# Narrow attentions: TensorE makes the scores of the batch three ahead in the middle of its slot, behind the first half of the product with the values, and no longer at the slot's end

## What is computed

```python
def attention(q, k, v, mask):
    scores = jnp.einsum('bhqd,bhkd->bhqk', q, k) / jnp.sqrt(jnp.float32(HD))
    scores = scores * mask - 10000.0 * (1.0 - mask)
    probs = jax.nn.softmax(scores, axis=-1)
    return jnp.einsum('bhqk,bhkd->bhqd', probs, v)
...
x = hidden_states + attn_out
ln_out = layernorm(x, ln2_s, ln2_b)
q = ln_out @ w_q + b_q
kv = encoder_states @ w_kv + b_kv
...
x = x + cross_out
```

## Time and profile before

| | |
|---|---|
| median of 3 runs | 2136.84 us |
| the profiled execution: its time, its span | 2138.01 us, 2136.3 us |
| TensorE matmuls busy (share of the span) | 1944.2 us (91%) |
| VectorE, ScalarE, GpSimd busy | 1261.8, 1085.0, 516.4 us |
| mean granted TensorE clock | 0.96 |
| first group of slot 0, last half of a product with the values, on TensorE, start | 40.66 us, 357.66 us |

### The profile page before, as it was taken

The page is one execution under the profiler, slowest core; times in us unless marked ns, Lnnn a source line. Parts: engine busy times, 40 slices in busy tenths (PEclk is TensorE's granted clock), DMA queues, the critical chain, the costliest instruction groups (busy, mean ns, idle before and its releaser), DMA issues. The chain is left out here.

```text
span 2136.3 us, 40585 instructions
## 1 busy us (share of the span) xinstructions
PE 1944.2 (91%) x15496; PEld 1692.5 (79%) x15496; DVE 1261.8 (59%) x2546; ACT 1085.0 (51%) x2920; POOL 516.4 (24%) x346
## 2 busy tenths in 40 slices
PE   6999996999999999999899999999988986898974
PEld 4677764997999999999699999999978984566653
DVE  6888886235645555555465555555552364888883
ACT  3787877545443344443453344334446543566653
POOL 3555453544200000000240000000005514324220
PEclk9999998999999999999999999999998997899986
DMA  5000001300000000002200000000020000000000
GB/s 188 2 2 2 2 2 42 117 1 6 6 6 5 0 5 5 5 5 90 74 6 1 5 5 5 5 0 5 29 89 1 1 1 1 1 11 6 6 11 10
DMA packets 29534, 40.72 MB, mean 19 GB/s; under 512 B 1923, under 2 KB 21477, under 8 KB 29157
## 3 DMA queue, kind: packets, MB, share of 16 engines
q1 hardware_dynamic: 29412, 39.06, 5.4%
HBM read 32.76 MB, written 2.10 MB: 16 GB/s over the span
## 5 line engine op out<-in xcount | busy, mean ns | idle before, releaser
L761 DVE TENSOR_TENSOR w_head_lo<-banks,w_head_hi 128x512 fp32r<-128x512 f32 x128 | 88.1, 691 | 249.5 <-ACT w_head_hi L673 241.9
L692 ACT ACTIVATE arena<-banks 128x512 f32<-128x512 f32 x128 | 74.9, 597 | 295.1 <-PE banks L551 291.0
L727 DVE TENSOR_TENSOR arena<-banks,cols 128x512 f32<-128x512 f32 x128 | 88.6, 692 | 227.0 <-PE banks L118 226.8
L470 POOL TENSOR_TENSOR w_hT_lo<-arena,w_hT_hi 128x512 fp32r<-128x512 f32 x16 | 20.9, 1306 | 821.0 <-ACT w_hT_hi L647 821.0
L685 ACT ACTIVATE arena<-banks,arena 128x129 f32<-128x129 f32 x512 | 181.3, 376 | 39.5 <-DVE arena L741 39.5
L964 POOL TENSOR_TENSOR arena<-arena 128x1024 f32<-128x1024 f32 x64 | 150.4, 2373 | 162.2 <-DVE arena L1250 162.2
L673 ACT ACTIVATE w_head_hi<-banks 128x512 fp32r<-128x512 f32 x128 | 76.5, 598 | 196.1 <-PE banks L561 196.0
L1168 ACT ACTIVATE arena<-arena 128x128 f32<-128x128 f32 x512 | 163.5, 397 | 1.8 <-DVE arena L1259 1.6
L116 PE MATMUL banks<-w_wo_lo,w_head_hi 128*128 128x256 f32 x512 | 148.6, 290 | 1.3 <-DVE w_head_lo L761 1.3
L116 PE MATMUL banks<-w_hT_lo,w_hi 128*128 128x256 f32 x512 | 146.6, 286 | 0.0
L116 PE MATMUL banks<-w_kv_lo,w_hi 128*128 128x256 f32 x512 | 145.2, 284 | 0.2
(11 more groups left out here) (299 smaller groups left out, 5702.9 us busy)
## 6 DMA issues: line engine op xcount, KB each, us to landing
arena<-in_L_xattn_wq SPq DMA_DIRECT2D x8, 512.0 KB, 4.9
arena<-in_L_xattn_wk SPq DMA_DIRECT2D x8, 512.0 KB, 6.0
arena<-in_L_xattn_wv SPq DMA_DIRECT2D x8, 512.0 KB, 6.9
arena<-in_L_xattn_wo SPq DMA_DIRECT2D x8, 512.0 KB, 9.5
arena<-ctx_t SPq DMA_DIRECT2D x16, 256.0 KB, 2.5
x<-in_x SPq DMA_DIRECT2D x4, 512.0 KB, 6.6
ctx_t<-in_ctx_t SPq DMA_DIRECT2D x1, 2048.0 KB, 11.7
arena<-in_L_xattn_w SPq DMA_DIRECT2D x2, 1024.0 KB, 12.8
```

Source lines behind the costliest of these rows:

```text
L692: act.activation(probT[:, b, :, :], bank[5 + b][:, :].rearrange("p (h q) -> p h q", h=HG), ACT.Copy).then_inc(probT_ok, 1)
L727: dve.tensor_tensor(qT[:, h:h + 2, :], bank[use % 2][:, :].rearrange("p (h t) -> p h t", h=2), core.col(bias, g * HG + h, 2)[:, :, None].t ...
L761: dve.tensor_tensor(head_lo[:, two, :], bank[5 + half][:, :].rearrange("p (h t) -> p h t", h=2), head_hi[:, two, :], ALU.subtract).then_in ...
```

## The change

In TensorE's slot `scores(n + 3)` moves from the last place to the place behind `weigh_values(n, 0)`. Nothing is added or removed, and the lists of the other engines are the same.

```diff
                 prob_transpose(n, 2)
                 weigh_values(n, 0)
+                if n + 3 < NU:
+                    scores(n + 3)
                 if even and r + 2 < NR:
                     project_q(r + 2, 1)
                 if not even and r + 2 < NR:
...
                 prob_transpose(n, 3)
                 if not even and r + 2 < NR:
                     project_v(r + 2, 1)
-                if n + 3 < NU:
-                    scores(n + 3)
```

## The result

| | before | after |
|---|---|---|
| median | 2136.45 us (20 runs) | 2140.57 us (20 runs) |
| profiled execution, span | 2136.3 us | 2138.1 us |
| period of a pair of slots | 20.4 us | 20.7 us |

The ratio is 1.0018, with a 95% interval of 1.0011 to 1.0025: slower by 3.9 us by the ratio (the two medians differ by 4.1), clear of no change, and just inside the line of 4.3 us that the prediction drew. The forecast was 2141.5 us, the range 2138 to 2145.5. The periods in the table are those of the ordinary pairs; two pairs are longer in both kernels (see "Why the prediction was right").

A forecast was written before the change was run, and what follows sets the result against it. TensorE was taken as the bound, though not alone. Delays of 0.46 + 0.04 less 0.20 saved make +0.30 us per ordinary pair, +4.7 in all on 2136.84: 2141.5 us, range 2138 to 2145.5.

The forecast's parts named there:

- The bound, and VectorE: Slot pairs: TensorE bounds, though not alone; ending VectorE's 1.54 us wait for scores gives TensorE nothing.
- Term 1: Even slot's end: scores delay `copy_q` and so the odd slot's first transpose, 0.46 us plus 0.04 per pair.
- the walk: New even slot, step by step from T2 to the odd slot's T0: 6.44 us, before 5.98.
- Term 2: TensorE's slots: two changes of the array's shape fall away per slot; only the odd slot's 0.20 us saving counts.
- The open point: Mid-slot, W0 directly ahead of S: 1.01 us taken unchanged, bounds 0.20 less and 0.20 more.
- the rival of a free entry: Mid-slot: scores load while W0 drains, saving up to 0.20 us in 29 slots; 2135.7 us; chance 0.12, free or nearly so.
- the rival of a saving that doesn't come: Shape changes in the slots: the 0.10 us steps are spent elsewhere, delay alone costs 7.6 us; 2144.4 us, chance 0.13.
- The sum: All slots: +0.87 for r = 0, 12 x 0.30, +0.40 for r = 13, -0.19 in slot 28; together +4.7 us.
- the prediction's step that nothing waits behind the odd slot: Odd slot's end: ScalarE has 2.54 us to spare at the next T0, so the 0.20 us saving counts.
- The rival of the clock: Slot 1: a 2.2 us gap lowers TensorE's clock, +1 to +1.7 us, time 2142.5 to 2143.2; chance 0.22.
- The chances: Whole kernel, against a 0.2% line (4.3 us): slower 0.64, same 0.34, faster 0.02; the forecast itself 0.45.

The follow-up runs named there:

- e2: Scores moved behind `weigh_values(n, 0)` in even slots only, against the kernel before; 2144.53 us, ratio 1.0035.
- e3: The full change, with `copy_q` also moved on ScalarE to the odd slot behind `copy_probs(n - 1, 3)`, against the kernel before; 2131.38 us, ratio 0.9971.
- e1: Scores moved behind `weigh_values(n, 0)` in odd slots only, against the kernel before; 2133.28 us, ratio 0.9982.
- e5: Scores moved ahead of `prob_transpose(n, 3)` in both slots, against the kernel before; 2135.63 us, ratio 0.9997.
- e6: Scores moved between `prob_transpose(n, 2)` and `weigh_values(n, 0)`, against the kernel before; 2138.96 us, ratio 1.0010.
- e9: Scores moved ahead of `prob_transpose(n, 2)` in both slots, `copy_q` left at the even slot's end, against the kernel before; 2122.63 us, ratio 0.9934.
- e4: The kernel before with only `copy_q` moved on ScalarE to the odd slot, against the kernel before; 2136.45 us, ratio 0.9999.
- e7: Scores moved ahead of `weigh_values(n, 0)` and `copy_q` moved on ScalarE to the odd slot, against the kernel before; 2128.13 us, ratio 0.9962.

## Why the prediction was right

**The bound, and VectorE.** That earlier scores give TensorE nothing through VectorE held: VectorE's wait for line 1042 went, others took its place, and the reciprocal ahead of the division started 1.15 us behind W1 in both kernels (113.22 to 114.37, 114.41 to 115.56).

**Term 1**, the delay of the odd T0, held step by step: the walk gave 6.44 us from T2, the profile has 113.85 - 107.41 = 6.44. The step from T0 to W0 was put at 4.09 and is 117.92 - 113.85 = 4.07. e2 shows the term alone (+0.50 per pair, as summed), and e3 its cause. The wait ahead of T0 was announced as 0.65 and reads 0.50: I had counted it from the point where the next group would have started, 1.73 behind PO's start, and the profile counts it from PO's end, 1.89 behind. The delay is the same.

**Term 2**, 0.20 us in the odd slot, came out at 0.19: from W0 to the next T0 it was 123.02 - 116.74 = 6.28 us and is 124.01 - 117.92 = 6.09. The open point, W0 directly ahead of S, came out at 1.01 us (107.97 to 108.98), the value taken. That ends the rival of a free entry (S at 0.85 or less behind W0) and the rival of a saving that doesn't come; e1's time and the periods of e1 and e5 agree with both. The Trainium skill ("TensorEngine Tiling (Array Packing)", section "Tiling Modes") says that a change of the tiling mode drains the engine. The trace agrees as far as it reaches: behind W0 the weight loads of S start with its own matmuls at 108.98, after 0.20 us without a load, as those of Q1 behind W0 did before:

```profile
108.98 0.74 PEld L1042 LDWEIGHTS banks<-arena 32*128 32x128 f32 x16 [0.20 <-issue]
```

How the 0.2 us is to be counted stays open. By the rule one change per slot falls away (six before, five after), which would be 0.2 us per change. Counting only the steps between the whole array and quarters, two fall away (six before, four after) at 0.1 us each, and then W0 to S costs nothing of its own. No run has S or W0 next to its own kind of quarters, which would tell the two apart. What is shown is that a group alone on quarters costs its neighbours some 0.2 us.

**The sum.** A pair was +0.30; measured 20.71 - 20.43 = +0.28. The prediction took all twelve pairs as alike, and two are not. In slots 10 and 18 ScalarE takes square roots (line 1180) ahead of the exponentials, with two loads of its tables of 1.28 us each, and is late for the next T0 already before the change. T0 of slot 10, before:

```profile
143.78 0.63 PE L1052 MATMUL banks<-ident,arena 128*128 128x128 f32 x4 [0.17 <-ACT arena L1175]
```

and after:

```profile
145.24 0.63 PE L1052 MATMUL banks<-ident,arena 128*128 128x128 f32 x4 [0.35 <-ACT arena L1175]
```

There the prediction's step that nothing waits behind the odd slot fails: the 0.2 us saved is lost in a longer wait, and the pair goes from 20.78 to 21.26 us, +0.48. For the two pairs that is 0.36 us more than the sum had; the other ten cost 0.02 less each. From T0 of slot 0 to T0 of slot 28 the changed kernel takes 330.60 - 41.76 = 288.84 us, where before took 326.22 - 42.49 = 283.73: +5.1, predicted 4.9 (the sum without slot 28). Slot 1's T0 was to wait 2.2 us:

```profile
51.70 0.63 PE L1052 MATMUL banks<-ident,arena 128*128 128x128 f32 x4 [2.23 <-ACT arena L1175]
...
334.75 0.63 PE L1052 MATMUL banks<-ident,arena 128*128 128x128 f32 x4 [1.88 <-ACT arena L1175]
335.31 1.08 PE L1067 MATMUL banks<-arena 128*32 128x128 f32 x32
336.32 1.15 PE L1042 MATMUL banks<-arena 32*128 32x256 f32 x16
```

The second group is slot 28, where the profiled execution of before lost some 1.6 us to the lower clock. In this one S lasts 1.15 us there, at the full clock. That gain, slot 0 starting 0.73 us earlier, and later stages that were 1.5 us shorter without any edit take back most of the 5.1 us, though the last output projection ran 0.7 us longer; the spans differ by 1.8 us only. The medians of 20 runs differ by 4.1. The sum said 4.7; the interval, +2.4 to +5.3 us, holds it. Whether the 0.6 us between them is scatter or the clock at slot 28 is open: only profiled executions show that clock, and it fell in some of them and not in others.

**The rival of the clock** did not happen: in the four profiles with a wait of 2.2 us in slot 1 (the change, e2, e6, e9) the granted clock is 1.00 from 48 to 56 us. It was seen in one execution each, so it remains open how often it falls in other runs.

**The chances** put 0.64 on more than 0.2% slower, and the measured 0.18% lies just below that, in the outcome that had 0.34. The sum was so near the line that the side on which the result fell was chance; the mechanism was right. Whether the shares given to the clock (0.22) and to a lost saving (0.13) were too high, one result can't tell.

**What the prediction did not see** is how much the slot had to give. It read the 1.6 us of waits per pair as a fact of the bound and asked whether the move shortens them; it did not ask which place would fill them. Two places ahead, S is worth -24 us with `copy_q` moved.

## What to carry to other kernels

Where the bound engine waits inside its own list, a group that is ready early belongs ahead of the wait, not behind it: the scores cost 4 us behind W0, gained 15 us ahead of T2, and with one copy on ScalarE reordered 24 us there and 32 us further ahead in the even slots. Before a group is moved ahead of others on one engine, follow what stands behind those others on the engines that read them: here one copy waited for Q1 in a strict list and held back the emptying of a bank it had nothing to do with. Groups that use the array in quarters gain some 0.2 us when they stand next to each other, but a wait that can be filled is worth more: in the best version S stands apart from W0 again.

## What the runs showed of the hardware that was not expected

- A group on quarters of 128 by 32 directly followed by one on quarters of 32 by 128 costs no more than one followed by a group on the whole array: W0 takes 1.01 us from start to start ahead of S as ahead of Q1.
- Gaps on TensorE of the same length, at the same place in the program, had different outcomes for the clock. Nine profiles have a wait of 1.87 to 1.93 us ahead of T2 of slot 28. Behind it the granted clock fell to 0.50, the level of 1.2 GHz, in five (before, e1, e2, e4, e5) and stayed at 1.00, the level of 2.4 GHz, in four (the change, e3, e6, e7); among the waits of 1.88 us both occur (e1 and e5 fell, the change did not). Behind 2.23 us in slot 1 of the changed kernel it stayed at 1.00. The length of the gap alone does not tell.
